# Zero rows of the bucket buffers stored piece by piece during the first two rounds of a message passing kernel

## What is computed

```python
h = jnp.maximum(_layernorm(x, axis=-1), 0.0)
# inside the layer
h = x @ W_in2f.T
Wij = smu(f_ij @ W_f1.T + b_f1) @ W_f2.T + b_f2
Wij = Wij * rcut_ij[:, None]
x_ij = h[idx_j] * Wij
agg = jax.ops.segment_sum(x_ij, idx_i, num_segments=h.shape[0])
out = smu(agg @ W_o1.T + b_o1) @ W_o2.T + b_o2
# and outside
return x + out
```

## Time and profile before

| | us |
|---|---|
| median of 3 runs | 4690.14 |
| profiled execution | 4673.0 |
| its span, first to last instruction | 4671.3 |
| busy PE / weight loads / DVE / ACT / GpSimd (POOL) | 3674.7 / 2929.2 / 3210.1 / 1518.5 / 3132.1 |
| zero stores: 12 of 3612 KB each | 43.3 MB of 720.26 MB moved |

### The profile page before, as it was taken

The page is one execution under the profiler, slowest core; times in us unless marked ns, Lnnn a source line. Parts: engine busy times, 40 slices in busy tenths (PEclk is TensorE's granted clock), DMA queues, the critical chain, the costliest instruction groups (busy, mean ns, idle before and its releaser), DMA issues.

```text
span 4671.3 us, 120335 instructions
## 1 busy us (share of the span) xinstructions
PE 3674.7 (79%) x32823; PEld 2929.2 (63%) x32823; DVE 3210.1 (69%) x12188; ACT 1518.5 (33%) x4903; POOL 3132.1 (67%) x3158
## 2 busy tenths in 40 slices
PE   0417777788888888888888888888888888888788
PEld 0305555566666666666666666666666666666676
DVE  6406556577777777777777777777777777777665
ACT  0603333333333333333333333333333333333201
POOL 0007777777777777777777777777777777777600
PEclk9759999999999999999999999999999999999999
DMA  8684333355555555555555555555555555555476
GB/s 191 180 189 126 94 96 94 104 156 157 156 155 158 158 159 155 158 158 158 156 155 158 157 155 157 154 155 157 159 156 156 154 158 157 158 156 154 149 216 187
DMA packets 373005, 720.26 MB, mean 154 GB/s; under 512 B 82062, under 2 KB 132900, under 8 KB 372346
## 3 DMA queue, kind: packets, MB, share of 16 engines
q1 hardware_dynamic: 246476, 456.19, 36.2%
q0 software_dynamic: 100352, 207.33, 12.7%
q10 hardware_dynamic: 26082, 55.61, 5.0%
HBM read 450.43 MB, written 268.35 MB: 154 GB/s over the span
## 4 chain that ended last, share of the span: by engine, by line
POOL 33%; DMA 24%; issue 22%; DVE 10%; ACTq 5%; PE 3%; ACT 1%; DVEq 1%; POOLq 1%; SPq 0%
POOL sorted_rows L491 33%; DMA sorted_rows<-msg,row_idx 21%; DVE msg L779 4%; ACTq L536 4%; DMA seg<-sorted_rows 2%; PE p_seg L976 1%; DVE product L785 1%; DMA x_all<-in_x 1%; DVE row_idx L793 1%; DVE onehot L771 1%; DVE agg L815 1%; DVE act L762 1%; POOLq L489 1%; DVE pick L766 1%; PE p_pos L1036 0%
## 5 line engine op out<-in xcount | busy, mean ns | idle before, releaser
L491 POOL DMA_INDIRECT sorted_rows<-msg,row_idx x3136 | 3121.9, 996 | 1249.3 <-issue 1142.3
L976 PE MATMUL p_seg<-seg_hot,seg 128*128 128x112 f32 x7840 | 1031.6, 280 | 323.6 <-DVE agg L815 273.1
L976 PEld LDWEIGHTS p_seg<-seg_hot,seg 128*128 128x128 f32 x7840 | 940.0, 192 | 395.9 <-issue 215.7
L926 PE MATMUL p_z<-attr,w_f 128*128 128x512 f32 x1568 | 862.9, 633 | 262.0 <-DVE act L762 232.7
L587 ACT ACTIVATE msg<-node_p 128x4 f32 (+1 forms) x784 | 163.8, 209 | 2492.9 <-DMA sorted_rows<-msg,row_idx 2492.8
L594 ACT ACTIVATE hg<-p_h,weight 128x128 f32<-128x128 f32 x3136 | 893.1, 373 | 86.5 <-PE p_h L944 58.4
L793 DVE TENSOR_TENSOR row_idx<-place,earlier 128x4 int32<-128x4 f32 x784 | 129.0, 165 | 1108.7 <-DMA sorted_rows<-msg,row_idx 1103.0
L933 PEld LDWEIGHTS p_w<-w_f,act 128*128 128x128 f32 x6272 | 826.9, 192 | 20.7
L933 PE MATMUL p_w<-w_f,act 128*128 128x128 f32 x6272 | 828.5, 275 | 0.0
L950 PEld LDWEIGHTS p_pos<-onehot,not_before 128*128 128x128 bf16 x3136 | 191.7, 98 | 849.1 <-DVE onehot L771 529.4
L944 PE MATMUL p_h<-win,pick 128*128 128x128 bf16 x9408 | 669.6, 222 | 4.1 <-DMA win<-h 4.1
(11 more groups left out here) (92 smaller groups left out, 1555.1 us busy)
## 6 DMA issues: line engine op xcount, KB each, us to landing
seg<-sorted_rows SPq DMA_DIRECT2D x784, 322.5 KB
ends<-ends SPq DMA_DIRECT2D x392, 256.0 KB
sorted_rows<-msg,row_idx POOLq DMA_INDIRECT x3136
sorted_rows<-zero_rows ACTq DMA_DIRECT2D x12, 3612.0 KB
win<-h SPq DMA_DIRECT2D x392, 96.0 KB
attr<-in_attrT SPq DMA_DIRECT2D x392, 80.0 KB
h<-h_parts SPq DMA_DIRECT2D x28, 336.0 KB, 2.7
x_all<-in_x SPq DMA_DIRECT2D x1, 5376.0 KB
```

The costliest lines, as they stand in the source:

```text
L491: pool.indirect_dma_start(out=sorted_rows[:, :], out_offset=bass.IndirectOffsetOnAxis(ap=row_idx[:, slot, k:k + 1], axis=0), in_=msg[:, sl ...
L926: pe.matmul(p_z[:, :], w_f1[:, :], attr[:, q, v * UNIT:(v + 1) * UNIT], start=True, stop=True).then_inc(s_z, 1)
L976: last = pe.matmul(p_seg[v][:, 0:NODE_P], seg[:, slot, k, 0:F], seg_hot[:, v, k, :], start=(k == 0), stop=(k == CAP_T - 1))
```

## The change

The zero stores keep their bytes, their order by buffer and their queue. `fill(b, part)` now stores one eighth of a buffer: 14 buckets x 64 x 2064 bytes. One such store stands at the head of a group of four units: groups 3 to 10 of round 0 for buffer 0, 11 to 18 for buffer 1, groups 3 to 10 of round 1 for buffer 2. GpSimd no longer waits for buffer 0 ahead of the first unit but at mid round (ahead of unit 56). Until then the scatters of round 0 may run beside the zero stores of the same buffer, which is harmless as long as no bucket has more than 384 rows; so DVE takes a copy of the counts in unit 57 into one more row of `counts`, shifted so that more than 384 (or less than 128) sends the kernel to the general path. For that, DVE's loop over round 0 is split at group 14 and that group written out; GpSimd's loop is split there too, and ACT's where the stores end.

```diff
-        counts = sb("counts", [1, rounds, BUCKETS])
+        counts = sb("counts", [1, rounds + 1, BUCKETS])
...
-                    pool.wait_ge(s_zero[st.rnd_of(1) % BUFS], 16 * 4)
+                    if 0 < st.rnd_of(1) < BUFS:
+                        pool.wait_ge(s_zero[st.rnd_of(1)], 16 * FILLS)
...
+                if rnd == 0:
+                    with pool.Fori(PEEL, MID) as i:
+                        for c in range(BODY):
+                            step(Beat(rnd, i, c))
+                    pool.wait_ge(s_zero[0], 16 * FILLS)
+                with pool.Fori(MID if rnd == 0 else PEEL, ROUND // BODY) as i:
...
-            def fill(b):
-                per = BUCKETS // 4
+            def fill(b, part):
                 whole = buf_view[b].rearrange("(l n) f -> l (n f)", l=BUCKETS)[:, FILLED * ROW:CAP * ROW].rearrange(
                     "l (a z) -> l a z", z=ZERO_ROWS * ROW)
-                for k in range(4):
-                    act.dma_start(whole[k * per:(k + 1) * per, :, :],
-                                  zero_rows[k * per:(k + 1) * per, :].unsqueeze(1).to_broadcast(
-                                      [per, fill_rows // ZERO_ROWS, ZERO_ROWS * ROW])).then_inc(s_zero[b], 16)
-
-            act.wait_ge(s_x, 16 * 3)
-            fill(0)
+                act.dma_start(whole[bass.ds(part * FILL_L, FILL_L), :, :],
+                              zero_rows[0:FILL_L, :].unsqueeze(1).to_broadcast([FILL_L, fill_rows // ZERO_ROWS, ZERO_ROWS * ROW])
+                              ).then_inc(s_zero[b], 16)
+
             act.wait_ge(s_quot, 1)
             act.dma_start(weight[:, :], t["weight_col"]).then_inc(s_weight, 16)
...
             loop(act, phase_a, n_groups, 4)
-            fill(1)
-            fill(2)
...
+            fills_in = {0: ((0, PEEL), (1, PEEL + FILLS)), 1: ((2, PEEL),)}
             for rnd in range(rounds):
                 for c in range(BODY * PEEL):
                     step(Beat(rnd, None, c))
-                with act.Fori(PEEL, ROUND // BODY) as i:
+                for b, lo in fills_in.get(rnd, ()):
+                    with act.Fori(lo, lo + FILLS) as i:
+                        fill(b, i - lo)
+                        for c in range(BODY):
+                            step(Beat(rnd, i, c))
+                with act.Fori(lo + FILLS if rnd in fills_in else PEEL, ROUND // BODY) as i:
...
+                if half:
+                    last = dve.scalar_tensor_tensor(counts[:, rounds, :], p_pos[0][0:1, 0:BUCKETS], CAP / 2 + FILLED / 2 - (FILLED - (CAP - FILLED) / 2),
+                                                    seed_row[:, 0, :], ALU.add, ALU.subtract)
                 last.then_inc(s_place, 1)
```

More of the change, by code:

```diff
@@ L85, in build @@
     ZERO_ROWS = 4
+    FILLS = 8
+    FILL_L = BUCKETS // FILLS
+    MID = ROUND // BODY // 2
     h3 = nc.dram_tensor("h3", [n_pad, PARTS * F], BF16, kind="Internal")
@@ L327, in bucket, with beats @@
                 return self.i * BODY + (self.c - back - SEG_LAG + ROUND)
-        def beats(eng, step, lag):
+        def beats(eng, step, lag, half=False):
             for rnd in range(rounds + 1):
@@ L332, in beats @@
                     step(Beat(rnd, None, c))
-                with eng.Fori(PEEL, ROUND // BODY) as i:
+                lo = PEEL
+                if rnd == 0 and half:
+                    with eng.Fori(PEEL, MID) as i:
+                        for c in range(BODY):
+                            step(Beat(rnd, i, c))
+                    for c in range(MID * BODY, (MID + 1) * BODY):
+                        step(Beat(rnd, None, c))
+                    lo = MID + 1
+                with eng.Fori(lo, ROUND // BODY) as i:
                     for c in range(BODY):
@@ L505, in _ @@
                     step(Beat(rnd, None, c))
-                with pool.Fori(PEEL, ROUND // BODY) as i:
+                if rnd == 0:
[4 more added lines that the diff above has]
+                with pool.Fori(MID if rnd == 0 else PEEL, ROUND // BODY) as i:
                     for c in range(BODY):
@@ L779, in message, with places @@
                 dve.tensor_tensor(msg[:, slot, :, 0:F], p_w[v][:, :, :], hg[:, v, :, :], ALU.mult).then_inc(s_msg, 1)
-            def places(n, v, slot, rnd):
+            def places(n, v, slot, rnd, half):
                 wait_for(dve, s_rank, n, 1, 1)
@@ L824, in step @@
                 if st.has(1):
-                    places(st.at(1), st.v(1), st.ring(1), st.rnd_of(1))
+                    places(st.at(1), st.v(1), st.ring(1), st.rnd_of(1),
+                           st.i is None and st.rnd == 0 and st.c == MID * BODY + 1)
                 if st.has_seg():
@@ L835, in step @@
                     totals(st.rnd - 1)
-            beats(dve, step, 2)
+            beats(dve, step, 2, half=True)
             dve.wait_ge(s_count, rounds)
```

## The result

The kernel after the change takes 4761.59 us in the median of 4 runs (4754.65 to 4767.52), the kernel before beside it 4690.23 (4686.88 to 4690.92). The ratio is 1.0153, 95% interval 1.0135 to 1.0171: slower by 1.5%, where 4562 us had been forecast. The profiled execution took 4767.52 us, its span is 4765.7 us.

The account below looks back on a forecast made before the run. Time was taken as first scatter's start, 3136 scatters at GpSimd's pace, and a 251 us tail. Terms -1.5 - 3.6 - 124.7 + 1.5 = -128.3 us gave 4545 for the profiled execution, 4562 for the median; 8-in-10 range 4553 to 4580.

Parts of the forecast that it names:

- The start: Before the first unit: without the zero stores there, first gelu and first scatter come 129.8 us earlier.
- 0.38 us each: ACT's queue in rounds 0 and 1: each zero piece finds it empty and holds ACT only 0.38 us.
- rival 1: ACT's queue: each piece holds ACT 11.1 us, half a full-queue store; 83 us lost, 4645 us; chance 0.05, in part included.
- the second: ACT's queue: each piece holds ACT 22.18 us, about 4911 us; slower once loss per piece passes 5.8 us; chance 0.02.
- GpSimd's pace: Scatters beside zero stores: 981 ns against 977 undisturbed, costing 1.5 us in all, 7.7 at most.
- half a piece needs 10 alone and perhaps 13 beside the units: DMA in rounds 0 and 1: us for a new zero piece to drain, within about 20.5 us per four units.
- DMA room in round 1: Round 1: 157 GB/s plus 89 for zero pieces is 246, against 239 moved earlier; cost 0, at most 5 us.
- rival 4: Rounds lose by bandwidth: 7.7 + 5 + 5 us of uncovered dips, 4578 us; chance 0.09 together with rival 3.
- rival 3: First unit gated by something else, such as slow attribute loads (9.3 us): gain 108, 4582 us; chance 0.09 with rival 4.
- the nearest case: First six units, 343 to 373 us, beside the old stores' tail: same traffic, scatters 981 ns, DMA 239 GB/s.
- The wait at mid round 0: GpSimd ahead of unit 56, on s_zero[0]: eighth piece issued some 80 us earlier, needs 13, so no wait.
- the count in unit 57: DVE: one small instruction in a step where DVE waits 2.0 us; general path not triggered.

Follow-up runs that it names:

- e1: Kernel after the change with the 14 source rows of each zero store read from partitions 0, 8, ..., 104 instead of 0 to 13: 4585.61 us, ratio 0.9792.
- e3: Kernel before, zero stores in their old places but cut into 24 of 14 rows, all read from partitions 0 to 13: 4949.12 us, ratio 1.0568.
- h5: Kernel after the change with spread source partitions and buffer 2's pieces moved to round 0: 4564.58 us, ratio 0.9736.
- h6: Kernel after the change with spread source partitions and pieces of half the size, twice as often: 4562.19 us, ratio 0.9727.
- h7: Kernel after the change, still adjacent source partitions 0 to 13, with pieces of half the size, twice as often: 4699.53 us, ratio 1.002.
- e5 to e8: Four variants of the changed kernel: spread with buffer 2 in round 0; spread halves; adjacent halves; spread with both. 6054.1, 6063.16, 6042.26, 6072.07 us beside 6175.03 for before.
- g5 to g8: The same four variants of the changed kernel run a second time: 5913.57, 5923.14, 5905.1, 5921.81 us beside 6025.31 for before.
- h5 to h8: The same four variants of the changed kernel run a third time: 4564.58, 4562.19, 4699.53, 4561.92 us beside 4687.92 for before.
- g5: Second run of the changed kernel with spread source and buffer 2's pieces in round 0: 5913.57 us, ratio 0.9817, beside 6025.31 for before.

## Why the prediction was wrong

- The start: right. The sum of the steps gave the first gelu at 204.9 and the first scatter near 213; they came at 205.28 and 213.61. The root began at 118.31 in place of 119.73, the bias copies took 5.62 us in place of 10.36, and the node stage ended at 195.7 as worked out.
- "0.38 us each" on ACT's queue: right, 0.33 to 0.40. Rivals 1 and 2 both looked for the loss in this hold; it isn't there, although the pieces did drain more slowly than one per 20 us, for which rival 1 gave the hold a few tens of us. The point from which the second decided, a loss over 5.8 us per piece, does hold for the loss that came: 207 / 24 = 8.6 us per piece.
- GpSimd's pace: right. 984 ns per scatter in 320 to 790 us of the kernel after, against 977 before. The nearest row gave this term well, and this term alone.
- **The step that failed** is "half a piece needs 10 alone and perhaps 13 beside the units". It took the rate of the old stores for the new ones by their bytes. But the source had changed with the cut: 28 partitions had become 14 adjacent ones (`zero_rows[0:FILL_L, :]` in the diff). A piece took 25.1 to 28.1 us in place of 13, longer than the 20.5 us of a group. e1 (one slice changed, 4585.6 us) and e3 (85 GB/s with nothing beside it) show that this is the cause of 169 us. Even the spread pieces of e1 took 15.3 to 18.2 us beside the units, so the 13 was low at the old rate too.
- With it fell "DMA room in round 1" ("Cost 0, at most 5") and rival 4. They took 239 GB/s from the earlier trace rows as what the engines can move, and added up GB/s. With the new rows a share of 0.78 moved only 137 GB/s, where 0.82 had moved 183.
- A second thing was missing, smaller: what the loads meet. The forecast asked who waits behind the issue on ACT's queue, not what stands in the DMA engines ahead of SP's loads. The earlier trace rows had the number, a first attribute load from 213.81 to 223.09, 9.3 us; it was priced once, for the first unit in rival 3, and not as one that each group would meet. The chain of waits of before has another, from the stretch that the prediction took for the nearest case, beside the last of the old zero rows:

```profile
343.02 12.29 DMA win<-h
```

  With spread partitions this is the 34 us of round 1 (13.81 and 14.16 us for the attributes), and h5 and h6 take it away in two ways.
- The rule of the Trainium skill ("DMA: Bandwidth & Descriptors", section "Issuing engines are not separate DMA queues") that transfers of all issuing engines end on the same 16 DMA engines was named and set aside, since "the scatter pace hardly changed". The late loads agree with it (22.22 us in place of 2.1); that the gain must come back as slower rounds does not follow, since h6 kept it with the same bytes. The scatters' pace was the wrong row to weigh it by: a scatter's length doesn't show how late its message is. The loads' landings do.
- The wait at mid round 0 and the count in unit 57: right, neither shows a gap of its own (GpSimd's idle times before the scatters of units 56 and 57 are 0.30 us). The stalls follow the loads of a group, not unit 56.

h6 has 0.9727 of before, 4562 us on 4690 with an interval of 4554 to 4571, which holds the forecast of 4562. So the sum stood for a kernel whose zero stores keep the old rate and are short enough for the loads behind them; that the two numbers agree within a microsecond is luck.

## What to carry to other kernels

When a transfer is cut or moved, price its rows anew: read the source's slice, not only the bytes, since 14 adjacent partitions gave 283 ns per row and 14 spread ones 145. Then hold two numbers against each other: rows per DMA engine times ns per row, against the lead of the loads that are issued behind them (64 x 0.28 = 18 us in the change, against 12.7), and the time of all that is stored per step against the step. The product comes out too low: the longest load took 23.2 us where it is 18 (the change), 14.9 where it is 64 x 0.145 = 9.3 (e1) and 9.2 where it is 32 x 0.145 = 4.6 (h6), and e1 still lost 34 us in round 1. The second comparison would have caught h7, where 32 x 0.28 = 9 is under the lead, but two half pieces need 25 us of a group of 20.5. An issue that returns in 0.33 us says nothing of either.

## What the hardware showed beside this

- The source partitions decided the rate of a store by a factor of two: 85 GB/s for 14 adjacent partitions, 171 for 14 in steps of 8, 183 for 28 adjacent ones.
- The spread source costs the issuing queue more: e1's pieces held ACT 0.84 us each, the adjacent ones 0.33; GpSimd had no gap from it in e1's round 0.
- SP's issues of attributes and edge ends took 3.2 and 3.6 us in the median (390 to 676 us), 4.2 at most, in place of 0.34 in round 0 of the kernel after, while an adjacent piece of ACT's queue was in the engines; in e1 the same issues took at most 2.4.
- The same kernel before took 6175, 6025 and 4688 us beside e5 to e8, g5 to g8 and h5 to h8. In g5's trace PE and DVE have pauses of 1 to 4 us that the profile puts on nothing but issue. In 2000 to 2500 us its DVE instructions took as long as in h5 (271.70 us for 1064, 371.63 for 1430), and its matmuls 131 ns in place of 109 (379.97 us for 2899, 421.29 for 3866) at a granted clock of 0.85 in place of 1.00. The cause stays open.
